# One of four expert sums folded in early, nine experts combined by a matrix of ones

## What is computed

```python
probs = softmax(x @ router_weight.T); topw, topi = top_k(probs, 8)
topw = topw / topw.sum(-1)
xe[e, pos] = x of the tokens that chose e          # 64 experts, 128 slots each, 1024 tokens
g, u = split(xe @ gate_up_proj[e])                 # 256 -> 2 x 96
ye = (silu(g) * u) @ down_proj[e]                  # 96 -> 256
y[token] = sum over its 8 experts of topw * ye     # the combine
out = x + gb * y
```

## Time and profile before

| | |
|---|---|
| median of 3 runs (lowest to highest) | 326.91 us (326.49 to 331.33) |
| profiled execution, its own time | 328.12 us |
| its span, first to last instruction | 326.3 us |
| PE busy | 282.3 us, 87% |
| DVE busy | 205.4 us, 63% |
| POOL busy | 159.6 us, 49% |
| ACT busy | 158.0 us, 48% |
| mean granted clock of PE | 0.945 of full |

### The profile page before, as it was taken

The page is one execution under the profiler, slowest core; times in us unless marked ns, Lnnn a source line. Parts: engine busy times, 40 slices in busy tenths (PEclk is TensorE's granted clock), DMA queues, the critical chain, the costliest instruction groups (busy, mean ns, idle before and its releaser), DMA issues.

```text
span 326.3 us, 7222 instructions
## 1 busy us (share of the span) xinstructions
PE 282.3 (87%) x2034; PEld 205.6 (63%) x2034; DVE 205.4 (63%) x616; ACT 158.0 (48%) x459; POOL 159.6 (49%) x157
## 2 busy tenths in 40 slices
PE   7999999789988997967669279999999999999950
PEld 3575677457645774655334158788888887778840
DVE  4397775888578867620650017667777779981396
ACT  3457296428832883245350025666666665690000
POOL 2700000005445455554747704788888888887000
PEclk9999999999999999699958859999999999999995
DMA  7980399999999999722929765789999999767952
GB/s 231 277 255 3 134 337 334 367 382 263 285 303 256 293 287 299 206 82 71 318 96 296 199 165 135 140 156 160 159 155 169 194 160 152 88 76 124 334 171 97
DMA packets 65752, 66.95 MB, mean 205 GB/s; under 512 B 4957, under 2 KB 62626, under 8 KB 65728
## 3 DMA queue, kind: packets, MB, share of 16 engines
q1 hardware_dynamic: 54976, 51.29, 55.5%
q0 software_dynamic: 10752, 15.37, 25.4%
HBM read 36.98 MB, written 30.15 MB: 206 GB/s over the span
## 4 chain that ended last, share of the span: by engine, by line
PE 54%; issue 17%; DVE 14%; ACT 6%; DMA 5%; SPq 2%; another core or an unknown queue 0%; ACTq 0%; DVEq 0%
PE bank L1132 12%; PE bank L1146 7%; PE bank L1123 4%; PE bank L884 4%; PE bank L960 3%; PE bank L958 3%; DVE arena L1515 3%; PE bank L944 3%; PE bank L915 2%; DMA arena<-sum 2%; PE bank L955 2%; PE bank L896 2%; PE bank L1140 2%; PE bank L912 2%; PE bank L990 2%
## 5 line engine op out<-in xcount | busy, mean ns | idle before, releaser
L583 POOL DMA_INDIRECT slot_rows<-stage x48 | 48.1, 1003 | 38.3 <-issue 9.6
L1132 PE MATMUL bank<-arena,stage 128*128 (+1 forms) x256 | 54.4, 335 | 0.7 <-ACT stage L785 0.7
L601 POOL DMA_INDIRECT sum<-kz,stage x28 | 43.2, 1543 | 9.5 <-issue 8.0
L785 ACT ACTIVATE stage<-bank 128x256 f32<-128x256 f32 x64 | 24.5, 383 | 38.2 <-PE bank L1123 29.2
L1132 PEld LDWEIGHTS bank<-arena,stage 128*128 128x128 f32 x256 | 41.3, 194 | 2.0 <-issue 0.9
L1146 PE MATMUL bank<-arena,stage 96*128 (+1 forms) x128 | 40.3, 397 | 0.0
L1274 DVE TENSOR_REDUCE rmax<-bank 128x2 f32<-128x512 f32 (+1 forms) x48 | 30.7, 686 | 4.6 <-PE bank L915 3.2
L837 PE MATMUL bank<-onesb 128*128 128x512 bf16 x81 | 25.2, 469 | 9.4 <-DMA slot_rows<-rows,slot_idx 6.9
L649 ACT ACTIVATE arena<-bank 128x512 f32<-128x512 f32 x48 | 26.8, 599 | 7.0 <-PE bank L960 5.3
L1464 DVE SCALAR_TENSOR_TENSOR stage<-stage,bank 128x96 f32<-128x96 f32 x64 | 16.1, 252 | 20.6 <-ACT stage L795 11.5
L570 POOL COPY stage<-slot_idx 128x16 uint32<-128x16 uint32 x2 | 0.4, 196 | 57.7 <-DMA sum<-zero_row 55.8
(11 more groups left out here) (184 smaller groups left out, 590.3 us busy)
## 6 DMA issues: line engine op xcount, KB each, us to landing
slot_rows<-zero_row SPq DMA_DIRECT2D x8, 1040.0 KB, 12.6
stage<-slot_rows SPq DMA_DIRECT2D x64, 130.0 KB
arena<-in_gate_up SPq DMA_DIRECT2D x8, 768.0 KB
sum<-zero_row SPq DMA_DIRECT2D x4, 1152.0 KB, 12.2
arena<-sum SPq DMA_DIRECT2D x16, 256.0 KB, 6.0
arena<-in_gate_up SPq DMA_DIRECT2D x4, 864.0 KB
arena<-in_down SPq DMA_DIRECT2D x4, 768.0 KB
arena<-in_gate_up SPq DMA_DIRECT2D x4, 672.0 KB
```

The source lines that it names most:

```text
L583: pool.indirect_dma_start(slot_rows, bass.IndirectOffsetOnAxis(ap=idx[:, t, k:k + 1], axis=0), src[:, t, :], None, bounds_check=SLOTS - 1, ...
L601: pool.indirect_dma_start(sums[a], where, ye_ring[e % RING], None, bounds_check=ACCROWS - 1, oob_is_err=True, compute_op=ALU.add).then_inc ...
L785: nc.scalar.activation(xeT[:, j % 2, :], bank[j % 2][:, 0:HC * CAP], ACT.Copy).then_inc(a_xeT, 1)
L1132: last = mm(bank[2 + q % 2][:, 0:GU + 1], xeT[:, q % 2, k * CAP:(k + 1) * CAP], expert_w[:, s - 1, k * (GU + 1):(k + 1) * (GU + 1)], start ...
```

## The change

- `FOUR = 24`: experts below 24 go to sum e % 4, from 24 on to e % 3. So the fourth sum is complete with the add of expert 23, its sixth.
- SP loads the fourth sum (four loads) after the slot loads of experts 0 to 31 and before those of 32 on; the load waits for the sum's last add.
- VectorE folds the fourth sum into x among the experts (`fold_fourth`): a multiplication by the gate and an addition to x for each sequence, eight operations of 128x512, one behind each of the steps 28, 31, ... 49. The even ones wait for the load of their sequence.
- Nine experts (55 to 63) are combined by the matrix of ones, 55 by POOL. The end has three sums: 4 + 4 x 4 = 20 operations. `fold_order` sorts them by their last expert.
- VectorE's experts are written out from 0 to 67, with constants in place of registers. The waits for the ring are on the same add, 16 experts before.
- `keep_warm(44, ...)` becomes `keep_warm(60, ...)`.

```diff
+    FOUR = 24
-    NPICK = 8
+    NPICK = 9
 ...
         def sum_of(e):
-            return e % NACC
-        fold_order = [(ADDED + n) % NACC for n in range(NACC)]
+            return e % NACC if e < FOUR else e % (NACC - 1)
+        fold_order = sorted(range(NACC - 1), key=lambda a: max(e for e in range(ADDED) if sum_of(e) == a))
 ...
-            with sp.Fori(1, 6) as i:
-                load_eight(i)
-            sp.dma_start(token_sb, token_row.broadcast_to([P, TOK])).then_inc(s_tr, 16)
-            with sp.Fori(6, E // GRP) as i:
-                load_eight(i)
-            for a in fold_order:
+            def load_sum(a):
                 sp.wait_ge(added[a], 16 * adds_before(ADDED, a))
                 for b in range(B):
                     sp.dma_start(part[:, a, b, :, :],
                                  sums[a][b * S:(b + 1) * S, :].rearrange("(t p) h -> p t h", p=P)
                                  ).then_inc(sum_ld[a][b], 16)
+            with sp.Fori(1, 4) as i:
+                load_eight(i)
+            load_sum(NACC - 1)
+            with sp.Fori(4, 6) as i:
+                load_eight(i)
+            sp.dma_start(token_sb, token_row.broadcast_to([P, TOK])).then_inc(s_tr, 16)
+            with sp.Fori(6, E // GRP) as i:
+                load_eight(i)
+            for a in fold_order:
+                load_sum(a)
 ...
-            keep_warm(44, bank[4])
+            keep_warm(60, bank[4])
 ...
-                    if not first:
-                        dve.wait_ge(added[q % NACC], 16 * (4 * i + (-3 if j < 3 else (j - 3) // NACC - 3)))
+                    if s - 3 >= RING:
+                        a = sum_of(s - 3 - RING)
+                        dve.wait_ge(added[a], 16 * adds_before(s - 3 - RING + 1, a))
 ...
+            def fold_fourth(n):
+                b = n // 2
+                s3 = part[:, NACC - 1, b, :, :]
+                ts = slice(TPB * b, TPB * b + TPB)
+                if n % 2 == 0:
+                    dve.wait_ge(sum_ld[NACC - 1][b], 16)
+                    link(V.tensor_tensor(s3, s3, gbB[:, b:b + 1, :].broadcast_to([P, TPB, H]), ALU.mult))
+                else:
+                    link(V.tensor_tensor(x_sb[:, ts, :], x_sb[:, ts, :], s3, ALU.add))
 ...
-            for s in range(E - RING, E + 4):
+            for s in range(E + 4):
+                if s < E and s % RING == 0:
+                    clear()
                 if s < E + 3:
-                    expert_steps(s // RING, s % RING, False, s >= E, s - 3 >= ADDED)
+                    expert_steps(s)
+                if FOUR + 4 <= s and s % 3 == (FOUR + 4) % 3 and (s - FOUR - 4) // 3 < 2 * B:
+                    fold_fourth((s - FOUR - 4) // 3)
```

More of the change, by code:

```diff
@@ L440, in _ @@
                 load_slots(0, j, True)
+            def load_sum(a):
+                sp.wait_ge(added[a], 16 * adds_before(ADDED, a))
+                for b in range(B):
+                    sp.dma_start(part[:, a, b, :, :],
+                                 sums[a][b * S:(b + 1) * S, :].rearrange("(t p) h -> p t h", p=P)
+                                 ).then_inc(sum_ld[a][b], 16)
             def load_eight(i):
@@ L1448, in _, with expert_steps @@
             slots(B - 1, (1,), B + 1, 1)
-            def expert_steps(i, j, first, last_, own=False):
-                s = RING * i + j
+            def expert_steps(s):
+                j, first, last_ = s % GRP, s < GRP, s >= E
+                own = s - 3 >= ADDED
                 if not last_:
-                    dve.wait_ge(xe_ld[j % GRP], 16 * (RING // GRP * i + j // GRP) + 16)
-                    V.tensor_copy(meta[:, 0:3, bass.ds(s, 1)],
-                                  xe[:, j % GRP, H:H + 3].rearrange("p (c o) -> p c o", o=1)).then_inc(v_meta, 1)
+                    dve.wait_ge(xe_ld[j], 16 * (s // GRP) + 16)
+                    V.tensor_copy(meta[:, 0:3, s:s + 1],
+                                  xe[:, j, H:H + 3].rearrange("p (c o) -> p c o", o=1)).then_inc(v_meta, 1)
                 if not (first and j < 1) and not (last_ and j > 0):
@@ L1470, in expert_steps @@
                     dve.wait_ge(a_w, s - 2)
-                    if not first:
-                        dve.wait_ge(added[q % NACC], 16 * (4 * i + (-3 if j < 3 else (j - 3) // NACC - 3)))
-                    V.tensor_scalar(ye_ring[(j - 3) % RING], bank[6 + q % 2][:, 0:H], gatew[:, q:q + 1],
-                                    meta[:, 1, bass.ds(s - 3, 1)],
+                    if s - 3 >= RING:
+                        a = sum_of(s - 3 - RING)
+                        dve.wait_ge(added[a], 16 * adds_before(s - 3 - RING + 1, a))
+                    V.tensor_scalar(ye_ring[(s - 3) % RING], bank[6 + q % 2][:, 0:H], gatew[:, q:q + 1],
+                                    meta[:, 1, s - 3:s - 2],
                                     ALU.mult, ALU.mult).then_inc(v_ye, 1)
```

## The result

The changed kernel is slower: 1.032 times the kernel before, with a 95% interval of 1.026 to 1.039. Beside each other on one chip the medians were 337.4 and 328.6 us. The forecast was 340.0 us, a ratio of 1.040.

The account below looks back on a forecast made before the run. POOL's adds and VectorE's final sums ended last, PE having 7.5 us of slack; 13.9 - 1.0 + 1.9 + 2.7 + 0.4 = 17.9 us shift made PE end last, 13.1 us over the span: 340.0 us, range 333.5 to 345 (0.80).

Parts of the forecast that it names:

- the stop: At step 28 VectorE's first fold waits for expert 23's add and the sum's load, shifting the next step 13.9 us.
- PE's work done ahead and its half clock: Around the wait at step 28: PE work done meanwhile gives back 1.0 us, resuming at half clock loses 1.9 us.
- further folds: The seven folds after the first, among VectorE's expert steps: 0.70 us less 0.31 idle each, 2.7 us in all.
- ninth comparison: VectorE's token comparison for the added expert: 0.73 us, partly covered by a step's idle 0.31, so 0.4 us more.
- product with ones: PE's combine behind the experts: 216 matmuls for 192, 23.8 us, 2.6 us more, ending last at 334.7.
- last bank read to end: At the kernel's end, from VectorE's read of PE's last bank: 4.7 us, as in the kernel before.
- What stands behind it on SP: Slot loads from expert 32 on, queued behind the sum's loads, land before VectorE needs them, some 5 us after it resumes.
- POOL's slack: POOL's adds and the final sums end 13 us ahead of PE's path; landings up to 5.2 us cost nothing.
- The no-stop rival: Fourth sum already in at step 28; folds and comparison delay experts 3.5 us, run time 325.7 us; chance 0.06.
- Warm products: Before the experts, 60 instead of 44 delay nothing and gain 0; the other bound is a 1.1 us gain.
- The two rules: Skill's shared-port exclusion (4.5 us more) and DMA landing fit (stop 4.0 us shorter, 336.0 us), both set aside for profile rows.

Follow-up runs that it names:

- experiment 10: Changed kernel with 110 products of the matrix of ones on PE in step 30, during the stop; one run, experts' stretch 143.3 us against 146.8.
- experiment 2: Changed kernel with the fourth sum's load left early on SP but the folds moved behind steps 39 to 62; 1.043 times the kernel before.
- experiment 8: Changed kernel with eight experts instead of nine in the matrix of ones; one run, experts' stretch 143.5 us against 146.8.
- experiment 4: Changed kernel with FOUR = 16 in place of 24, load and folds left in place; 1.004 times the kernel before.
- experiment 1: Changed kernel with the fourth sum's load behind the slots of experts 0 to 39 and folds behind steps 39 to 62; 1.001 times the kernel before.
- experiment 9: Changed kernel with FOUR = 48, fourth sum loaded after all slot loads and folded after the last expert step; 0.997 times the kernel before.
- experiment 11: Kernel before with 76 warm products in place of 44; one run, experts' stretch 134.2 us against 135.5.

## Why the prediction was right, point by point

The place and the cause of the stop, its length and what sets the end were right. What stands behind them on SP, and POOL's room, was not, and some of that was luck, as said below.

In the changed kernel's steps against before's, each counted from the first meta copy:

| term | forecast | measured |
|---|---|---|
| step 28 to 29, over before's | 13.9 | 14.6 |
| PE's work done ahead and its half clock, to step 32 | -1.0 + 1.9 | +1.4; clock alone 1.5 (experiment 10) |
| further folds | 2.7 | 1.3 (to step 50) |
| ninth comparison | 0.4 | 0.0 |
| sum from step 28 on | 17.9 | 17.2 |
| drift before step 28 | 0 | -1.1 |
| product with ones | 23.8 | 23.75 |
| last bank read to end | 4.7 | 4.7 |
| stretch over before's | 13.1 | 11.3 |

*The stop.* Right in place, cause and size. Its parts were 3.76 us of landing (4.2 taken), 5.10 of load (4.7 taken), and POOL's lag, 6.3 us behind step 28 in this execution where the earlier trace rows had 5.8.

*What stands behind it on SP.* "They land before VectorE needs them, some 5 us after it resumes" was true in the changed kernel, and hid that SP's wait was a full stop of its own (experiment 2). The step priced the queue only in the presence of the other stop. That this cost the forecast nothing was luck: the two stops lay over one another.

*The folds.* 0.70 us less a step's idle 0.31 was the term mis-sized: a fold set VectorE back by up to 0.7 us, and it caught up most of that before the next. Six folds cost 1.3 us, 0.2 each.

*Before step 28.* The gain of 1.1 us was in no term, and it isn't shown to be of the change: other kernels whose code is the same up to there came to step 28 between 0.3 us (experiment 8) and 1.5 us (experiment 10) ahead of before.

*POOL's slack.* Here the prediction was wrong. It held that a landing up to 5.2 us costs nothing, three adds (5.54 us) less the usual 0.30 between two. But where an add waited for its own chain it began 0.8 us after the last landing event of the add before, in every trace (1.6 us at a few, the adds 28 and 49 above all), so the room is 5.54 - 0.8 = 4.7 us. Expert 29's add landed after 5.09 us, and that of expert 32 came 0.35 us late for it. Nor are nearly all landings shorter. Of the 9.3 us that POOL loses in the changed kernel the stop has 5.9 (add 26) and 1.4 (add 28), the chains 1.3 (adds 32, 36 and 40), and 0.5 an add that a fold held (see below).

It also counted 16 operations at the end, where all 20 ran one behind the other. The final adds begin 123.5 us after the first copy, so this path would have ended at about 140.3 (an estimate: 20 operations take 14.2 us in experiment 8, and 2.6 follow for the store), 6.5 us ahead of PE's, where 13 were forecast. That did not change the forecast, since PE's path stayed the longer.

*The no-stop rival.* It gave 325.7 us, a ratio of 0.996, with PE's path at the end. Experiment 4 (0.999 to 1.009) excludes that; experiment 1 (0.996 to 1.006) only just holds it. What is refuted by both is that the 1.85 us and the 3 us of POOL's path, 1.5% together, come free once the stop is gone.

*Warm products.* Right: with 60 the clock fell again by 186, and nothing was gained (the first add came 8.2 us after the first copy, 7.6 in before). 1.1 us had been given as the bound; with 76 the first add came 1.2 us sooner than in before.

*The two rules.* The add's landing of 3.76 us agrees with the rows and not with the fit of the Trainium skill ("DMA: Bandwidth & Descriptors", section "Anatomy of one DMA — SWDGE (gpsimd) path"), which gives 2.3. That fit is for DMAs that GpSimd issues; the prediction's 2.6 us for a load of the sum, which SP issues and which took 5.10, doesn't follow from it. The rule on VectorE and GpSimd was set aside too early. The operation held against it, at 287.92, did not lie in the midst of an add: it began 0.12 us before one ended and was over before the next began. See below for what the folds showed.

## What to carry to other kernels

A wait in a step written for one engine must be set against the time at which the slowest engine of the pipeline gets there, not against the step's number: POOL began the add of expert 23 6.3 us, some four steps, after VectorE had begun step 28, and the fold was timed in VectorE's steps. A queue that serves two purposes (slots and sums on SP) makes such a wait a second stop, which only shows when the first is taken away, so try each alone. A releaser that the profile names should be held against the time at which that engine or landing was done. And a buffer that is taken from a chain (four sums to three) costs room for the slowest landings, which a mean doesn't show.

## What the runs showed of the hardware

**A fold can hold an add, in one order.** All the changed kernel's accumulating adds but one took 1.54 to 1.57 us, and that one began just after a fold had begun. From its timeline of VectorE:

```profile
260.54 0.68 DVE L1518 TENSOR_TENSOR x_sb<-x_sb,arena 128x512 f32<-128x512 f32 x1
```

and of POOL:

```profile
260.61 2.02 POOL L608 DMA_INDIRECT sum<-kz,stage  x1 [0.66 <-issue]
```

With 0.61 us of the fold left as the add began the add took 2.02, with 0.46 left 1.87 (experiment 9, above), with 0.33 left 1.75 (experiment 4): 0.13 us less than the fold's rest was added. Folds are not the only operations beside which an add was longer: in experiment 11, which has none, the add at 272.13 took 1.65 and began with 0.23 us of a token comparison left. A fold that began while an add ran (0.02 to 1.5 us after its start, some fifty times in the traces) changed neither, and no fold took over 0.73 us. The Trainium skill ("SBUF — State Buffer", section "SBUF: two separate sides") says that of a VectorE operation with two SBUF inputs and a GpSimd one that reads SBUF, whichever starts first holds the shared ports for its whole instruction. The trace agrees where VectorE was first and doesn't where POOL was. The cost here is under 0.5 us for a fold, and for one fold in the changed kernel.

**An accumulating add lands later than a plain write.** The first write to each sum is plain. In the changed kernel these four landed 2.4 to 2.7 us after their start by the landing events, and were issued in 1.0 us each; no accumulating add of the same 128 KB landed in under 3.7, and each took 1.54 us to issue.

**A landing beside a burst.** An add of 128 KB lands 3.7 us after its start with little beside it; the adds of experts 25 to 27 in experiment 1, with 1 MB of loads and then eight slots beside them, took 7.0, 7.8 and 7.0 us; a slot load 3.2 us in the median of the changed kernel and about 6 behind four loads of a sum (experiment 2).
